# State space's tail in a four-layer block: gated sums taken from PSUM, one norm moved behind the program boundary, thirteen unread TensorE passes added

## What is computed

```
x = x + _L0_attn_a_ref(_layernorm(x), ...)
x = x + _L0_ffn_ref(_layernorm(x), ...)
x = x + _L0_attn_b_ref(_layernorm(x), ...)
x = x + _L0_ffn_ref(_layernorm(x), ...)

# the end of _L0_attn_b_ref (inner size 256, state size 64)
    y = (y - mu) * jax.lax.rsqrt(var + 1e-05)
    y = y @ W_si + b_si
    y = y + D * x_main
    y = y * jax.nn.sigmoid(gate)
    return y @ W_out + b_out

# _L0_ffn_ref: 16 experts, the best 2 of each token
    router_logits = jax.nn.sigmoid(x @ gate_w + gate_b)
    expert_values, expert_indices = jax.lax.top_k(router_logits, k=TOP_K)
    ...
    return x + _mlp(x, shared_wg, shared_wu, shared_wd) + expert_weighted
```

## Time and profile before

| | us |
|---|---|
| median of 3 runs | 809.27 |
| lowest and highest | 809.16, 810.39 |
| the profiled execution: time | 810.24 |
| the profiled execution: span, first to last instruction | 808.5 |

### The profile page before, as it was taken

One profiled execution on the slowest core, in us unless ns is written; L12 is line 12 of the kernel. 1 busy time (PEld: TensorE's weight loads), 2 busy tenths in 40 slices (PEclk: granted clock), 3 DMA queues, 4 the chain that ended last, 5 costly groups with the idle time before them and its releaser, 6 DMA issues. The chain is left out here.

```text
span 808.5 us, 14388 instructions
## 1 busy us (share of the span) xinstructions
PE 741.7 (92%) x5520; PEld 502.7 (62%) x5520; DVE 450.9 (56%) x1216; ACT 386.0 (48%) x476; POOL 423.7 (52%) x311
## 2 busy tenths in 40 slices
PE   2789999999999999999999998988799998678998
PEld 1456555655655655565565554977688864567887
DVE  5765665575675566566566611544654547555342
ACT  2346545555555655555555452353563444355421
POOL 3346765685675667648657664033535422254343
PEclk9799999999999999999999999999999999899999
DMA  2000000000000000000000001622223000033232
GB/s 65 8 1 1 8 2 1 8 1 1 9 1 1 8 1 1 9 1 2 1 1 12 17 2 39 155 84 84 71 84 105 1 1 0 24 101 102 75 99 79
DMA packets 29752, 25.56 MB, mean 32 GB/s; under 512 B 10162, under 2 KB 21236, under 8 KB 29684
## 3 DMA queue, kind: packets, MB, share of 16 engines
q1 hardware_dynamic: 29684, 24.64, 10.4%
HBM read 23.32 MB, written 1.31 MB: 30 GB/s over the span
## 5 line engine op out<-in xcount | busy, mean ns | idle before, releaser
L378 POOL TENSOR_TENSOR all_x<-all_x,at_probs 128x1024 f32<-128x1024 f32 (+3 forms) x128 | 216.4, 1691 | 35.7 <-ACT at_probs L453 21.1
L453 ACT ACTIVATE at_probs<-at_ring 128x1024 f32<-128x1024 f32 x144 | 147.2, 1023 | 114.1 <-PE at_ring L625 107.3
L498 DVE CUSTOM_DVE_ANT_0 at_ring<-at_ring,at_after_query 128x128 f32<-128x128 f32 (+3 forms) x256 | 119.5, 520 | 74.2 <-PE at_ring L590 74.2
L643 PE MATMUL at_out<-at_probs,at_k_nat 128*64 128x512 f32 (+3 forms) x768 | 140.3, 494 | 1.1 <-DVE a_attn_t L521 0.9
L1086 POOL TENSOR_TENSOR m_prod<-m_gate,m_wb 128x512 f32<-128x512 f32 x64 | 81.9, 1285 | 109.1 <-ACT m_gate L941 104.1
L378 POOL TENSOR_TENSOR all_x<-at_probs 128x768 f32<-128x768 f32 (+1 forms) x32 | 67.0, 2095 | 130.9 <-ACT at_probs L453 130.7
L995 DVE TENSOR_TENSOR m_hid<-m_prod,m_u 128x512 f32<-128x512 f32 x64 | 44.0, 687 | 88.5 <-POOL m_prod L1086 82.1
L643 PEld LDWEIGHTS at_out<-at_probs,at_k_nat 128*64 128x64 f32 x768 | 49.2, 136 | 69.9 <-issue 66.0
L494 DVE TENSOR_REDUCE at_half_max<-at_ring 128x2 f32<-128x1024 f32 x64 | 75.4, 1221 | 12.4 <-PE at_ring L590 12.4
L941 ACT ACTIVATE m_gate<-m_g 128x512 f32<-128x512 f32 x72 | 42.6, 598 | 79.3 <-PE m_g L853 78.8
L861 PEld LDWEIGHTS m_acc<-rest_wd,m_hid 128*128 128x128 f32 x576 | 76.5, 195 | 6.2
(11 more groups left out here) (234 smaller groups left out, 1282.8 us busy)
## 6 DMA issues: line engine op xcount, KB each, us to landing
m_wb<-m_wt_far SPq DMA_DIRECT2D x128, 128.0 KB, 2.9
all_x<-in_L_attn_a_x SPq DMA_DIRECT2D x8, 256.0 KB, 3.7
at_w_raw<-in_L_attn_a_W_qk SPq DMA_DIRECT2D x8, 128.0 KB, 2.6
out<-all_x SPq DMA_DIRECT2D x4, 256.0 KB, 3.3
a_room<-in_L_attn_a_W_out SPq DMA_DIRECT2D x1, 512.0 KB, 4.0
m_raw_wg<-in_L_ffn_experts_wg SPq DMA_DIRECT2D x1, 512.0 KB, 4.6
m_raw_wu<-in_L_ffn_experts_wu SPq DMA_DIRECT2D x1, 512.0 KB, 4.2
rest_wd<-in_L_ffn_experts_wd SPq DMA_DIRECT2D x1, 512.0 KB, 4.2
```

What stands on the lines that cost most here:

```text
L378: return pool.tensor_tensor(sums[:, :, a * P:b * P], left, right, ALU.add)
L453: act.activation(probs[:, :, slot * BANK:(slot + 1) * BANK], pair("S", unit, slot)[:, :, :], ACT.Exp, scale=BETA).then_inc(exp_done, 1)
L498: last = dve.tensor_tensor_reduce(out=sums_ps, in0=sums_ps, in1=after_query[:, BANK - w:BANK], scale=1.0, scalar=MASKED, op0=ALU.add, op1= ...
L643: last = pe.matmul(out_ps[rows(l), o:o + (b - a) * P], k_nat[g % 3][:, j, rows(l)], probs[:, l, at:at + (b - a) * P], start=(j == 0), stop ...
```

## The change

Four edits, all at the end of `state_space` but one. (1) VectorE's additions of the second half go in the order 4, 6, 5, 7; those of 5 and 7 write their sum back into the PSUM bank that they read, and VectorE's two multiplications read the sum from that bank, once all four additions are counted. (2) GpSimd's waits on `closed` follow the new order. (3) The norm of group 0 goes from the end of VectorE's queue in `state_space` to the head of its queue in the mixture: the filter in `interleave` no longer leaves it out. (4) TensorE gets 13 matmuls of 512 columns behind its last output tile. They write the transposes' bank, which nobody reads any more.

```diff
@@ mixture, interleave
             todo = [item for item in agenda(pieces, next_norm, tiles)
-                    if item[2] >= early or item[1] not in ("source", "statistics", "root", "norm")]
+                    if item[2] >= early or item[1] not in ("source", "statistics", "root")]
@@
 SSM_BANKS = 4
+WARM = 13
@@ state_space, GpSimd
-                for i in (1, 3, SETS, SETS + 2):
+                for i, n in ((1, 2), (3, 4), (SETS, SETS + 1), (SETS + 2, SETS + 2)):
                     h, b, c = out_tile(i)
-                    pool.wait_ge(closed, i + 1)
+                    pool.wait_ge(closed, n)
@@ state_space, TensorE
+                def busy(n):
+
+                    for _ in range(n):
+                        pe.matmul(turn_ps[:, :], v.w_hi[:, TAPS, 0:P], k.xhi[:, 0:BANK], start=True, stop=True)
...
                 outputs(1)
+                busy(WARM)
@@ state_space, VectorE
-                def add_out(i):
+                def add_out(i, to=None):
+
                     h, b, c = out_tile(i)
                     r = tokens(b, h)
                     dve.wait_ge(out_ready, i + 1)
                     dve.wait_ge(skipped, SETS * (h + 1))
-                    dve.tensor_tensor(z[c][:, r], z[c][:, r], bank("out", i)[:, :], ALU.add).then_inc(closed, 1)
-
-                def multiply(i, gates):
+                    dve.tensor_tensor(z[c][:, r] if to is None else to, z[c][:, r], bank("out", i)[:, :], ALU.add)\
+                       .then_inc(closed, 1)
+
+                def multiply(i, gates, added_up=None, sums=0):
                     h, b, c = out_tile(i)
                     r = tokens(b, h)
-                    dve.wait_ge(closed, i + 1)
+                    dve.wait_ge(closed, sums or i + 1)
                     dve.wait_ge(gate_done, gates)
-                    return dve.tensor_tensor(z[c][:, r], z[c][:, r], sg[c][:, r], ALU.mult)
+                    return dve.tensor_tensor(z[c][:, r], z[c][:, r] if added_up is None else added_up, sg[c][:, r], ALU.mult)
...
                 first.statistics(dve, 0, first_x)
-                for i in range(SETS, 2 * SETS):
+                for i in (SETS, SETS + 2):
                     add_out(i)
                 for i in (SETS + 1, SETS + 3):
-                    multiply(i, 2 * SETS)
-                first.norm(dve, 0, first_x)
+                    add_out(i, bank("out", i)[:, :])
+                for i in (SETS + 1, SETS + 3):
+                    multiply(i, 2 * SETS, bank("out", i)[:, :], 2 * SETS)
```

## The result

The changed kernel's median was 804.10 us over 4 runs (803.69 to 805.03), beside 809.21 for the kernel before (808.86 to 810.39, 4 runs): ratio 0.9939, 95% interval 0.9925 to 0.9953. The gain was 5.1 us where 3.3 were forecast.

The account below looks back on a forecast made before the run. VectorE, last ahead of the barrier, and TensorE's half clock behind it were taken as the bound. Barrier 1.89 plus clock 1.44 gave 3.33 us off 809.27: 805.9 us, range 804.7 to 807.8.

Parts of the forecast that it names:

- VectorE's tail, GpSimd: End of state_space: multiplications no longer block each other; VectorE ends at 688.45 instead of 689.44, GpSimd at 688.47 instead of 688.89.
- The thirteen passes: TensorE behind its last output tile: 0.231 us each, 3.00 us in all, ending last at 688.80; barrier 1.89 us earlier.
- The norm: Behind the barrier: its 1.33 us is covered by twelve product passes of 1.44 us, so costs nothing.
- The clock in the tail: Start of last mixture: TensorE's clock stays up, saving 1.26 us in product passes and 0.18 in the turn, 1.44 together.
- The whole tail: Barrier to ScalarE's copy: 1.89 us from the barrier plus 1.44 from the clock, 3.33 us, all let through.
- The change doesn't touch these stretches, so the same difference holds for the median: Later clock falls in the last mixture taken as unchanged, so 3.33 us comes off the median 809.27, giving 805.9.
- it fell twice more in it: Profiled execution, last mixture: two later clock falls of 3.3 us at half speed, worth up to 1.65 us each.
- Its mirror, one fall less, gives 804.3: Opposite of the third rival: one clock fall less in the mixture, 804.3 us; put within the range, no own chance.
- the fall at 700.9: Last mixture: clock fell after TensorE was nearly idle from 699.0 to 700.8; one of the two later falls.
- Rivals: VectorE still waits, 806.7 (0.10); passes don't hold clock, 807.4 (0.08); gain lost later, 807.6 (0.07); passes serialize, 811.1 (0.03).

Follow-up runs that it names:

- filled pair: Kernel before and changed kernel, both with unread matmuls only where TensorE has room in the mixtures (second filling): 806.10 and 802.86 us.
- filled pairs: Kernel before and changed kernel with unread matmuls ahead of routing-weight turns: first filling 808.98 and 805.71 us, second, with fewer places, 806.10 and 802.86.
- 14 later runs: The changed kernel repeated unfilled in two further sets: medians 806.68 us (9 runs) and 805.51 us (5 runs), mean 805.66.
- later sets: Measurements after the first four runs, with the unchanged kernel before run beside the others: mean of its 76 runs 808.80 us.
- two filled forms: Kernel before with unread matmuls ahead of routing-weight turns: at all four turns of both mixtures 808.98 us; only where TensorE has room 806.10 us.
- The changed kernel filled: Changed kernel with unread matmuls in both mixtures only where TensorE has room: 802.86 us (5 runs).

## Why the prediction was right or wrong

**VectorE's tail, GpSimd** (right): The forecast ends, 688.45 and 688.47, lie 2.65 and 2.67 us behind the end of the last output tile (685.80). Measured: 687.57 and 687.29, so 2.96 and 2.68 behind 684.61. The forecast's reason for no new wait, that TensorE had both last tiles done by 685.80, doesn't carry: the second addition was due at 685.29, before that. VectorE's 0.3 us more lie in two pitches: 0.85 us from the first addition to the second, which waited for tile 6, and 0.73 from the last addition to the first multiplication, instead of 0.60. TensorE, at 3.18, still ends last. Multiplications 0.69 and 0.68, as worked out, and 1.58 for the first with the sums in SBUF.

**The thirteen passes** (mis-sized a little): 3.00 us forecast from the end of the last output tile, 3.18 measured (684.61 to 687.79). The barrier moved by 1.71 us instead of 1.89. The 0.131 us per matmul of the Trainium skill (TensorE: Matmul & The Clock Gate, Back-to-back issue gap), cited in the forecast, is not what these took: 3.18 / 13 is 0.245 from end to end, and from start to start it is (3.25 - 0.40) / 12 = 0.24.

**The norm** (right): cover of 1.41 us for 1.33; taking it back costs 1.0.

**The clock in the tail** (right in the profiled pair, undersized in the filled one): 1.44 forecast, 1.43 between the two profiled executions. The filled pair's own trace shows 1.7, the medians 1.9: there the low stretch lasts until 694.6 and catches the whole turn.

**The whole tail**: 3.33 forecast; 3.14 and 3.42 in the traces, 3.24 and 3.27 in the medians of the filled pairs, 3.5 between the means of all unfilled runs. ScalarE's copy stands 5.56 us behind the last output tile, for 5.38 forecast.

**The step that failed** is "The change doesn't touch these stretches, so the same difference holds for the median", and with it the range. Their instructions are untouched indeed, but the falls in them are not the same from one execution to the next. The forecast also saw too few of them ("it fell twice more in it"): besides the tail's own, the kernel before had two in the last mixture and two in the first in its profiled execution; the changed kernel's first trace had one and one. I had priced one such fall (1.65 us: "Its mirror, one fall less, gives 804.3") and then set the low end at 804.7, above the very case I said was inside. A median of a few runs moves by more than one fall: the three medians of the same changed kernel are 804.1, 806.7 and 805.5. Of these two lie in the range, and so does the mean of 18 runs, 805.3. That the first four runs lay below it was in the main luck: of their gain of 5.1 us the tail is 3.1 to 3.4, and the 14 later runs gain 3.1 in all. What is not shown is that it was luck alone, since the fall at 700.9 was missing in all three traces of the changed kernel.

**Rivals**: none of the four occurred. The mirror that got no chance of its own, fewer falls, did.

## What to carry to other kernels

Where the granted clock falls in idle stretches that the change doesn't touch, cut the two traces at a row ahead of the change and a row behind it, and cost the three pieces apart: here 1.2, 3.1 and 1.8 us, of which the middle one is the change's and the last is in part open. One trace of each kernel doesn't settle it, nor does one median of four runs. To measure such a change more closely, first fill those stretches in both kernels with unread matmuls, but only as many as TensorE waits for anyway: eight in a gap of 0.85 us delayed the work behind them by 0.8, and three such places cost all that the fillings won. Work that stands ahead of a barrier on the engine that arrives last belongs behind it, if another engine has cover for it there.

## What the runs showed of the hardware

Beside GpSimd, VectorE's multiplication took 0.68 us with one operand in PSUM and, when it came second, 1.58 to 1.78 with both in SBUF; when GpSimd came second, its own took 1.73 to 1.74 instead of about 1.3. The clock was low for at least 13.7 us of the first 48 us in every trace. The clock's falls are not the kernel's alone: single runs of one unchanged program spread over 4.0 us (806.75 to 810.79 for 76 runs of the kernel before in the later sets), and those of its two filled forms over 1.0 (11 runs) and 0.8 us (7 runs). The changed kernel filled still spread over 1.8 (801.20 to 803.02, 5 runs). TensorE was idle for 5.2 us ahead of the barrier and the clock was low behind it in all three traces; after 3.26 us it was low behind it, or fell within a us, in all seven; after 2.06 us it stayed up in the one trace there is.
